# Layer norms of a transformer block spread over up to three periods, with fewer small steps on Pool and the turns behind V's products

## What is computed

```python
def _adaln(x, c, lw, lb, gw, gb, bw, bb):
    g = (c @ gw + gb)[:, None, :]
    bt = (c @ bw + bb)[:, None, :]
    return _ln(x, lw, lb) * (1.0 + g) + bt
attn_in = _adaln(x, cond, ln1_w, ln1_b, g1_w, g1_b, b1_w, b1_b)
x = _attn(attn_in, attn_in, sa_wq, sa_wkv, sa_wo, sa_bo) + x
cross_in = _adaln(x, cond, ln1_w, ln1_b, g1_w, g1_b, b1_w, b1_b)
ctx_n = _ln(context, ca_lnc_w, ca_lnc_b)
x = _attn(cross_in, ctx_n, ca_wq, ca_wkv, ca_wo, ca_bo) + x
ffn_in = _adaln(x, cond, ln2_w, ln2_b, g2_w, g2_b, b2_w, b2_b)
h = jax.nn.gelu(ffn_in @ ff_w1 + ff_b1, approximate=False)
x = h @ ff_w2 + ff_b2 + x
```

## Time and profile before

| | before |
|---|---|
| median of 3 runs | 1227.95 us (1226.4 to 1228.6) |
| the profiled execution | 1228.63 us, span 1226.8 us |
| granted TensorE clock, mean | 0.973 |
| PE busy | 1121.1 us |
| DVE, ACT, Pool busy | 906.9, 630.3, 701.5 us |

### The profile page before, as it was taken

The page is one execution under the profiler, slowest core; times in us unless marked ns, Lnnn a source line. Parts: engine busy times, 40 slices in busy tenths (PEclk is TensorE's granted clock), DMA queues, the critical chain, the costliest instruction groups (busy, mean ns, idle before and its releaser), DMA issues.

```text
span 1226.8 us, 18768 instructions
## 1 busy us (share of the span) xinstructions
PE 1121.1 (91%) x6888; PEld 793.8 (65%) x6888; DVE 906.9 (74%) x1128; ACT 630.3 (51%) x861; POOL 701.5 (57%) x538
## 2 busy tenths in 40 slices
PE   3469899888999999999999999999999999985998
PEld 3346666665666666666665666666666666653997
DVE  2467787687787788788888887788778878865443
ACT  3235555555555555556556555555555555665221
POOL 1367575666666666676777666666666666763000
PEclk9689999999999999999999999999999999997999
DMA  5111211221112111211112111211121111110001
GB/s 167 34 35 36 64 31 42 49 54 46 36 35 69 36 36 36 61 40 27 27 36 65 35 35 35 66 36 35 36 65 35 36 35 47 41 35 1 18 18 35
DMA packets 65690, 52.37 MB, mean 43 GB/s; under 512 B 29120, under 2 KB 48576, under 8 KB 65344
## 3 DMA queue, kind: packets, MB, share of 16 engines
q1 hardware_dynamic: 63712, 49.59, 16.3%
q10 hardware_dynamic: 1888, 1.59, 0.4%
HBM read 15.22 MB, written 2.10 MB: 14 GB/s over the span
## 4 chain that ended last, share of the span: by engine, by line
PE 76%; DVE 9%; issue 5%; ACT 5%; POOL 2%; DMA 2%; SPq 1%; ACTq 0%; POOLq 0%; DVEq 0%
PE ps L725 16%; PE ps L590 11%; PE ps L592 10%; PE ps L591 10%; PE ps L703 5%; PE ps L713 5%; PE ps L678 4%; PE ps L790 4%; PE ps L684 4%; PE ps L680 4%; PE ps L682 4%; DVE neg_max L888 3%; DVE w_lo L875 1%; ACT z L418 1%; PE ps L600 1%
## 5 line engine op out<-in xcount | busy, mean ns | idle before, releaser
L460 ACT ACTIVATE probs<-ps 128x1024 f32<-128x1024 f32 x256 | 262.4, 1026 | 216.4 <-PE ps L684 196.8
L888 DVE TENSOR_REDUCE neg_max<-ps 128x2 f32<-128x1024 f32 x256 | 299.2, 1220 | 48.3 <-PE ps L703 48.3
L361 POOL TENSOR_TENSOR acc<-acc,probs 128x1024 f32<-128x1024 f32 x128 | 304.8, 2381 | 16.6
L369 POOL TENSOR_TENSOR eo<-tmp 128x512 f32<-128x512 f32 x64 | 92.6, 1447 | 250.2 <-DVE tmp L914 248.9
L725 PE MATMUL ps<-probs,v 128*64 128x512 f32 x1024 | 230.7, 592 | 0.0
L356 POOL TENSOR_TENSOR acc<-probs 128x1024 f32<-128x1024 f32 x64 | 152.7, 2386 | 90.5 <-ACT probs L460 90.5
L725 PEld LDWEIGHTS ps<-probs,v 128*64 128x64 f32 x1024 | 73.6, 137 | 145.7 <-issue 145.7
L914 DVE TENSOR_TENSOR tmp<-ps,rope 128x1024 f32<-128x1024 f32 x128 | 151.1, 1215 | 15.3 <-PE ps L592 15.3
L703 PE MATMUL ps<-hi 64*128 64x512 f32 x512 | 114.7, 438 | 18.2 <-ACT v L492 9.0
L590 PE MATMUL ps<-xn_hi,w_hi 128*128 128x512 f32 x256 | 109.7, 428 | 21.6 <-issue 10.2
L678 PE MATMUL ps<-max_rows,pick 64*128 64x512 f32 x512 | 111.4, 424 | 4.6 <-DVE o_lo L901 3.5
(11 more groups left out here) (107 smaller groups left out, 2224.4 us busy)
## 6 DMA issues: line engine op xcount, KB each, us to landing
lo<-eo SPq DMA_DIRECT2D x512, 64.0 KB, 2.0
w_raw<-pack_dram SPq DMA_DIRECT2D x16, 192.0 KB, 3.4
x<-x_dram SPq DMA_DIRECT2D x4, 512.0 KB, 11.0
w_raw<-pack_dram SPq DMA_DIRECT2D x8, 256.0 KB, 4.2
max_rows<-neg_max SPq DMA_DIRECT2D x128, 2.0 KB, 2.0
w_raw<-w_dram SPq DMA_DIRECT2D x2, 1024.0 KB, 5.6
out<-x SPq DMA_DIRECT2D x4, 512.0 KB, 2.9
ctx_in<-ctx_dram SPq DMA_DIRECT2D x4, 384.0 KB, 3.7
```

The source lines that it names most:

```text
L361: pool.tensor_tensor(acc[:, g % 2, :, :], acc[:, g % 2, :, :], probs[:, i, :, :], ALU.add).then_inc(added, 1)
L460: act.activation(probs[:, i, :, :], score_ps(i), ACT.Exp, scale=SCALE).then_inc(exped, 1)
L888: dve.tensor_reduce(neg_max[:, g % 2, :, i], peak_ps(i), AX.X, ALU.max, negate=True).then_inc(maxed, 1)
```

## The change

The integer guess and three Newton rounds become two ACT instructions on 128x4 (Ln, then Exp with scale -0.5: guess_rstd) and one Newton round with the two steps for the centre (refine_rstd, six steps). A table norm_at gives each norm the periods of its statistics, rows and turn. Norms 1 to 3 and 8 to 11 do all three in one odd period ("at once"): ACT then makes guess and rows ahead of high_o. The context norms (periods 5, 6, 7 and so on to 17, 18, 19) and norms 12 to 14 (59 to 65) take three periods, with the refinement behind Pool's last addition and the rows at the end of ACT's period. The turn becomes the last thing of PE's period, behind project, project_out and project_v; ACT converts behind keep_v. The first bank of the turn is now bank 1 and the second bank 7, so the next score waits for the first pair of conversions and peak 1 for the second. The low parts go from DVE to the head of Pool's next period; out_first goes. load_ctx is issued in the period of the rows. The waits of score and peak on ln_scaled swap their numbers with the banks, and the loops run two periods longer.

```diff
         def ln_ps(n, r):
-            return ps[:, (7, 6 if n == LAST else 1)[r], :]
+            return ps[:, (6 if n == LAST else 1, 7)[r], :]
...
-        stats_in = {-3: 1, -1: 2, 1: 3, 5: 4, 7: 5, 9: 6, 11: 7}
+        norm_at = {n: (2 * n - 5, 2 * n - 5, 2 * n - 5, True) for n in range(1, NB)}
         for b in range(NB):
-            stats_in[QUADS - 5 + 2 * b] = norm_of(X, 1, b)
-            stats_in[2 * QUADS - 5 + 2 * b] = norm_of(X, 2, b)
-        del stats_in[2 * QUADS + 1]
-        turned_in = {p + 1: n for p, n in stats_in.items()}
-
-        STATS = 2 * TT + 2
-        STEPS = 4 * NEWTON + 2
+            norm_at[norm_of(C, 0, b)] = (5 + 4 * b, 6 + 4 * b, 7 + 4 * b, False)
+            p = QUADS - 5 + 2 * b
+            norm_at[norm_of(X, 1, b)] = (p, p, p, True)
+        norm_at[norm_of(X, 2, 0)] = (PAIRS - 5, PAIRS - 4, PAIRS - 3, False)
+        norm_at[norm_of(X, 2, 1)] = (PAIRS - 3, PAIRS - 2, PAIRS - 1, False)
+        norm_at[norm_of(X, 2, 2)] = (PAIRS - 1, PAIRS, PAIRS + 1, False)
+        stats_in = {at[0]: n for n, at in norm_at.items()}
+        rows_in_period = {at[1]: n for n, at in norm_at.items()}
+        turned_in = {at[2]: n for n, at in norm_at.items()}
+        low_in = {at[2] + 1: n for n, at in norm_at.items()}
+
+        STATS = 2 * TT + 1
+        STEPS = 6
...
+        def refine_rstd(eng, n):
+            eng.wait_ge(ln_guess, 2 * n + 2)
+            eng.tensor_tensor(newton[:, :], rstd[:, :], rstd[:, :], ALU.mult).then_inc(ln_newton, 1)
...
+            eng.tensor_scalar(centre[:, :], newton[:, :], -1.0, None, ALU.mult).then_inc(ln_newton, 1)
...
             def period(p):
+                if p in low_in:
+                    norm_split(pool, low_in[p], 0)
+                    norm_split(pool, low_in[p], 1)
                 if is_pair(p):
                     add_probs(p, 1)
                     add_probs(p, 2)
                 n = stats_in.get(p)
-                if n is not None:
-                    invert_root(pool, n)
+                if n is not None and norm_at[n][3]:
+                    refine_rstd(pool, n)
                 if is_pair(p):
                     add_probs(p, 3)
+                if n is not None and not norm_at[n][3]:
+                    refine_rstd(pool, n)
                 if is_job(p + 4):
                     rotate(p + 4)
+                n = rows_in_period.get(p)
                 if n is not None and order[n][0] == X:
                     add_bias(n)
...
+            def guess_rstd(n):
+                act.wait_ge(ln_step, STATS * (n + 1))
+                act.activation(rstd[:, :], var_eps[:, :], ACT.Ln).then_inc(ln_guess, 1)
+                act.wait_ge(ln_guess, 2 * n + 1)
+                act.activation(rstd[:, :], rstd[:, :], ACT.Exp, scale=-0.5).then_inc(ln_guess, 1)
...
                 if is_pair(p + 2):
                     high_qk(p + 2)
+                n = stats_in.get(p)
+                at_once = n is not None and norm_at[n][3]
+                if at_once:
+                    guess_rstd(n)
+                    norm_rows(n)
                 if is_pair(p - 1):
                     high_o(p - 1)
                 if is_pair(p):
                     keep_av(p)
-                n = turned_in.get(p)
-                if n is not None:
-                    norm(n, 0)
-                    norm(n, 1)
-                if p in stats_in:
-                    norm_rows(stats_in[p])
-                if p % 2 == 1 and is_quad(u + 1):
+                if n is not None and not at_once:
+                    guess_rstd(n)
+                keeps_v = p % 2 == 1 and is_quad(u + 1)
+                if keeps_v:
                     keep_v(u + 1, 0)
                     keep_v(u + 1, 1)
+                if p in turned_in:
+                    norm(turned_in[p], 0)
+                    norm(turned_in[p], 1)
+                n = rows_in_period.get(p)
+                if n is not None and not norm_at[n][3]:
+                    norm_rows(n)
...
+            guess_rstd(0)
             norm_rows(0)
...
+            guess_rstd(LAST)
             norm_rows(LAST)
...
                 if r == 0:
                     pe.wait_ge(ln_rows, TT * (n + 1))
+                    p = norm_at[n][2] if n in norm_at else -1
+                    if p > 0:
+                        pe.wait_ge(av_kept, min(p + 1, PAIRS))
...
-                n = turned_in.get(p)
-                if n is not None:
-                    if is_pair(p):
-                        pe.wait_ge(av_kept, p + 1)
-                    norm(n, 0)
-                    norm(n, 1)
-                out_first = n is not None and order[n][0] == X
-                if not out_first and is_job(p + 4):
+                if is_job(p + 4):
                     project(p + 4)
                 if p % 2 == 0 and is_quad(u - 1):
                     project_out(u - 1, 0)
                     project_out(u - 1, 1)
-                if out_first and is_job(p + 4):
-                    project(p + 4)
                 if p % 2 == 1 and is_quad(u + 1):
                     project_v(u + 1, 0)
                     project_v(u + 1, 1)
+                n = turned_in.get(p)
+                if n is not None:
+                    norm(n, 0)
+                    norm(n, 1)
...
-            for p in range(FIRST, PAIRS + 1):
+            for p in range(FIRST, PAIRS + 3):
```

87 lines of the change are left out of this document (33 added, 54 removed).

## The result

The changed kernel takes 1192.84 us (median of 4 runs, 1192.72 to 1193.37) where the kernel before takes 1227.97 in the same comparison: a ratio of 0.9717, 95% interval 0.97 to 0.9733, so 35.1 us less. The forecast was 1197.0, with a range of 1184 to 1214. The profiled execution took 1192.72 us, 1.8 of them beyond its span of 1190.9.

A forecast was written before the change was run, and what follows sets the result against it. PE (TensorE) was taken as the bound, busy 1121.1 of 1226.8 us, with gains where it idles around norms. Stages summed to -34.2; 1 for port and 2 for clock left -31.2, so about 1197, range 1184 to 1214.

The forecast's parts named there:

- The turn: At the end of PE's period: costs 2.75 us, 3.5 where a weight split follows, with a score gap of 1.5 to 1.7.
- Periods 4 to 19: Stage with the four context norms: 269.71 us falls to 258.5, so 11.2 us less.
- A: Rival: half clock at every turn, the short way, losing 22 us instead of 2, so 1217; chance 0.10.
- C: Rival: a long half-clock stretch ends each turn, losing 44 us where 2 were taken, so 1239; chance 0.04.
- my term of 2: Allowance of 2 us for clock falling after gaps of 1.6 us at 13 turns, bounds 0 and 22.
- B: Rival: at-once norms come later, each us beyond DVE's 0.8 of slack costing one in seven norms: 1209; chance 0.09.
- Period 28: After an at-once cross norm, later high_o plus a weight split on DVE exceeds the slack: about 1.2 us late.
- the 0.7 in period 29: Cross norms: a weight split on DVE exceeds the slack by 0.7 us in period 29, likewise 0.7 in 34.
- The start: Start to period 1: 97.20 us falls by 9.2; first rows 2.0 later, period 0 from 20.52 to 11.4.
- The end: From period 60: 7.7 us less, 3.8 of it in periods 60 to 62; first down projection at 1127.0, not 1134.69.
- The port: DVE and Pool hindering each other once low parts move to Pool: 1 us, bounds 0 and 17.
- The context load and the root: Earlier context request removes 13.6 us of waiting; six Pool steps take 1.65 us instead of 3.9, plus 0.6 on ACT.

The follow-up runs named there:

- the end alone: Changed kernel with the last inverse guess ahead of norm 13's conversions and second feed-forward weight splits on ACT, those weights' low parts later on DVE: 1189.13 us.
- the guess first: Changed kernel with the guess of norm 0 as ScalarE's first work, ahead of the weight splits: 1192.11 us, ratio 0.9713.
- the low parts behind low_qk: Changed kernel with the norm's low parts back on DVE, behind low_qk at the end of DVE's period: 1242.13 us, ratio 1.0121.
- the turn between: Changed kernel with the turn of the spread norms (4 to 7, 12, 13) between project and project_v, conversions interleaved with V evictions: 1190.33 us.
- the split first: Changed kernel with ScalarE's weight split ahead of the V evictions and the turn's conversions in periods 11, 19, 27 and 33: 1187.53 us.
- the long root: Changed kernel with three Newton rounds again on Pool for norms 1 to 14, fourteen small steps instead of six: 1208.60 us, ratio 0.9847.
- the halves on the kernel before: Kernel before with one part alone: context asked for one period earlier, 1212.76 us; short root (Ln, Exp, one Newton round), 1221.39 us. Both together: 1209.53 us.

## Why the prediction was right, and where it missed

**The turn** (2.75 us, 3.5 with a weight split, a gap of 1.5 to 1.7) came as worked out: 1.62 to 1.63 at the score, released by the conversion. A turn shows in two periods together, over 2 x 15.31 = 30.62: 7 and 8 take 33.18, so 2.6; 11 and 12, with a split, 33.96, so 3.3. In the norms done at once it is less, 29 and 30 taking 32.72, so 2.1; why, I did not find out. Periods 4 to 19 fell 1.2 us further than their sum; 0.8 of this is no gain, since the split at the end of period 19 is paid in period 20, which I had counted in the stage before. The splits beside the statistics of periods 9 and 17, priced at 0.5 each, make the peaks of 10 and 18 0.76 us late.

**The clock.** Rivals A and C fell: behind the gap of 1.63 us PE kept full clock (1.00 over the period) in ten of eleven turn periods. In 28 a second gap of 2.02 us, at the peaks, followed, and the clock went to 0.51 for 3.4 us (last row of the windows), which is the 1.2 GHz level. That cost 1.7 us, so my term of 2 was about right in size, but for another place and another pattern, which is luck. It did not have to fall there: the kernels with the end alone and with the guess first have the same pair of gaps in period 28 and half clock with it, while those with the low parts behind low_qk and with the turn between have 1.63 and then 2.01 and 2.08 us, and keep 1.00 behind it. Period 28 of the latter:

```profile
513.41:531.35 17.94, 15.67 (x97) 10.52 (x97) 14.59 (x14) 9.55 (x15) 14.36 (x8) 1.00 0.13 30
```

Where that second gap goes, as with the split first, the clock stays at 1.00. The Trainium skill (TensorE: Matmul & The Clock Gate, HAM oscillation) warns of waits repeated in a loop, in a case where each is longer than the work between them; here one gap of 1.63 us in every second period, behind some 30 us of work, did not bring the half rate. Half clock was seen behind all single gaps of 3.9 to 4.8 us in the kernel with low parts at the end of DVE's period. No rule for the shorter ones comes out of these rows: a single 2.71 us in period 62 of the kernel before brought it, and one of 2.34 in period 60 with the long root did not.

**The at-once norms** (rival B, "each us beyond DVE's 0.8 of slack costs one"): the slack was mis-sized, on the safe side. DVE had done the work of period 29 at 554.54 and waited 1.81 us for PE's first peak tile of period 30, not 0.8, so B had 1 us more to go than I said:

```profile
553.33 1.21 DVE L924 TENSOR_TENSOR lo<-lo,hi 128x1024 fp32r<-128x1024 f32 x1
556.36 4.74 DVE L907 TENSOR_REDUCE neg_max<-ps 128x2 f32<-128x1024 f32 x4 [1.81 <-PE ps L738]
```

B's mechanism, peaks that wait for DVE after an at-once norm, was not reached, and no run shows it at work there. With 2.3 us more of Pool's steps DVE still waited 1.35 us ahead of those peaks. The 8.5 us that four norms lost in that kernel came by another way, which neither B nor the forecast had: the turn waited for keep_av, and half clock followed.

**Period 28** ("with a weight split on DVE it is over: about 1.2 us") is the step that failed in its reason. I summed DVE's own work and looked for what was late in high_o. What was late was w_hi on ACT, and w_lo then took 2.98 us beside Pool's add_bias. I had left w_hi where it was in my count: the split keeps its place behind the conversions in ACT's queue, and when the turn goes to the end of PE's period the conversions, and the split with them, go too. Moving high_o moved nothing that the time shows; moving the split gained 5.3 us in all. Its late place cost 2.0 us of gap and, by half clock over 3.40 us, 1.7 more: with the rest the period took 4.6 us more than 30 and 32, where I had 1.2. The sum for the stage (151.3, measured 151.41) held by luck, because errors of opposite sign met: the turns there cost 2.1 each and not 2.75, period 28 took 3.4 us more than I said, and nothing came of the 0.7 in period 29 (34 took 0.55 more, as said).

**The start** gained 11.2, not 9.2. The two ACT instructions on 128x4 took 0.20 and 0.21 us, at the lower bound of 0.2 and not at my 0.3, and the first rows started at 18.39, not at 19.8:

```profile
16.72 0.20 ACT L430 ACTIVATE rstd<-var_eps 128x4 f32<-128x4 f32 x1
16.96 0.21 ACT L432 ACTIVATE rstd<-rstd 128x4 f32<-128x4 f32 x1
18.39 1.09 ACT L440 ACTIVATE z<-x,centre,rstd 128x256 f32<-128x256 f32 x2 [1.23 <-DVE centre L256]
```

The first project started at 52.97, not at 54.4 (57.12 before). But 1.1 of the surplus of 2 us stood there before the first changed instruction: ACT's last weight split ahead of the rows, which both kernels have, started at 17.24 us before and at 16.11 after.

```profile
17.24 0.71 ACT L449 CAST w_hi<-w_raw 128x256 fp32r<-128x256 f32 x2
16.11 0.71 ACT L471 CAST w_hi<-w_raw 128x256 fp32r<-128x256 f32 x2
```

And as the start of period 0 differs by 1.9 us among kernels that begin alike, how much of the rest is the change's stays open.

**The end** gained 6.8, not 7.7, and larger errors hide in that. Periods 60 to 62 gave 4.4 us, not 3.8. From the start of period 63 the last project_out came after 21.6 us, where the prediction has 18.1, and the first down projection after 38.9, where it has 36.1: 2.8 too late. Behind that 1.3 came back, which the prediction names only for the lower end of its range: what follows took 90.8 us, not the 92.1 of before, at a granted clock of 1.00. Total(63) did come with no wait of its own, as forecast. "ACT's weight splits hold the inverse guess" named half of what stands there: norm 13's four conversions, 2.7 us, stand ahead of the splits, because its turn moved as well. I counted the new place of a turn in norm 14's case and missed it in norm 13's. The experiment on the end measured what this order costs: 3.7 us, or 4.1 at project_out in the rows.

**The port** (1 us, bounds 0 and 17): it was paid in one place that counts, period 28, where w_lo beside add_bias took 2.1 us more than alone, on the way to the late peaks. No run takes that part away by itself. Elsewhere it found slack: low_qk beside Pool's additions in period 30 takes 2.13 us and not 1.21, and nothing waits for it. The low parts no longer run on DVE; at the head of its period they cost 20.6 us. So the edit that the prediction gave a cost of 1 us and no gain is the dearer of the two parts that I took out of the changed kernel again (the short root: 15.8).

**The context load and the root** are the terms that the halves on the kernel before bear out: 14.9 and 6.3 us, 18.3 together.

## What to carry to other kernels

When a step is moved on one engine, list what stands behind its successors on every in-order queue, the unrelated work too: the two misses with a size (period 28, the end) were a weight split and an inverse that had stayed "where it was", behind conversions that moved. A long sum of waits on an engine with time to spare says little (43.9 us of them were worth 6.3), and a short one on the engine that feeds the bound can be worth its whole length (13.6 us gave 14.9). Price an element-wise step by its queue and its port, not by its speed alone: Pool's 1.3 us beat DVE's 0.69, for DVE's became 2.8 in the two periods where it had no time to spare. And one profile of a kernel is one draw of the clock: with equal gaps period 28 took 19.6 us in one kernel and 17.9 in another.

## What the runs showed of the hardware

- A DVE instruction with two SBUF inputs went from 0.69 to 2.8 us (128x512) and from 0.42 to 1.5 us (128x256, two in 2.98) beside Pool's additions of 2.5 us. A reduction from PSUM in the same stretch did not lengthen: four peaks took 4.61 us in period 28 and 4.74 in 30.
- An ACT activation on 128x4 takes 0.20 to 0.22 us, no more than one of Pool's small steps.
- Single PE gaps of 1.63 us, two periods or more apart, left the granted clock at 1.00 in ten cases. Two gaps, 1.63 and then 2.0 to 2.1 us with 4 us of work between them, came with 3.4 us of half clock in three kernels and with full clock in two.
- In five kernels with the same start, period 0 begins at 74.56 to 76.43 us, a spread of 1.9 us, as large as the smaller edits here are worth.
